# Two layers of attention and feed-forward on one core: the first chunk's q goes to its token layout inside the chip, and the loads behind it are re-ordered

## The reference

```
xn = layernorm(x)
x  = x + attention0(xn) + lora_experts(xn)     # layer 0
xn = layernorm(x)
x  = x + attention1(xn) + swiglu(xn)           # layer 1

attention0: q = xn @ Wqkv[:, :512]  (32 heads of 16), k and v of one shared head
            scores = q.k * scale + slope[h] * (pos_k - pos_q), causal
            out = softmax(scores) @ v  @ Wo
lora_experts: top 2 of 4 gates, rank 16
attention1: within a token, a 16 x 16 softmax of q (sum over heads) and k
swiglu:    (silu(xn @ gate) * (xn @ up)) @ down,  512 -> 1792 -> 512,
           gate, up and down are int32 weights with a scale per row
```

## Time and profile before

| | |
|---|---|
| Time, three runs | median 625.92 us (625.88 to 626.74) |
| Span of the profiled execution | 623.2 us; no separate time of that execution is given, so what lies around the span is taken from the median: 2.7 us |
| PE busy | 570.7 us (92%) |
| DVE, ACT, POOL busy | 461.3, 377.0, 351.7 us |
| Granted clock of PE, mean | 0.959 |
| DMA moved | 34.97 MB in 98942 packets |

### The profile page before, as it was taken

The page is one execution under the profiler, slowest core; times in us unless marked ns, Lnnn a source line. Parts: engine busy times, 40 slices in busy tenths (PEclk is TensorE's granted clock), DMA queues, the critical chain, the costliest instruction groups (busy, mean ns, idle before and its releaser), DMA issues.

```text
span 623.2 us, 14286 instructions
## 1 busy us (share of the span) xinstructions
PE 570.7 (92%) x5590; PEld 421.3 (68%) x5590; DVE 461.3 (74%) x1034; ACT 377.0 (61%) x703; POOL 351.7 (56%) x364
## 2 busy tenths in 40 slices
PE   4579583699999999999999999999999999999997
PEld 4466451467885668776968587858685876785783
DVE  4769874899999874899697748996986569354642
ACT  3287095847875478675757485858684776651240
POOL 6231595724655667674837574848576677542140
PEclk9987895599999999999999999999999999999999
DMA  8767799905054146001610160016001000000000
GB/s 207 152 95 78 123 237 217 170 2 54 2 54 87 37 68 70 3 4 35 88 17 5 35 86 4 4 35 88 1 5 52 18 1 9 28 2 2 35 1 34
DMA packets 98942, 34.97 MB, mean 56 GB/s; under 512 B 75548, under 2 KB 90044, under 8 KB 98876
## 3 DMA queue, kind: packets, MB, share of 16 engines
q1 hardware_dynamic: 76044, 24.58, 22.7%
q0 software_dynamic: 2352, 7.18, 5.7%
q10 hardware_dynamic: 20480, 2.31, 2.6%
HBM read 30.19 MB, written 8.39 MB: 62 GB/s over the span
## 4 chain that ended last, share of the span: by engine, by line
PE 68%; DVE 13%; SPq 8%; ACT 4%; issue 3%; DMA 2%; POOL 2%; ACTq 1%; DVEq 0%
PE B_bank L1266 27%; PE B_bank L1287 14%; PE A_bank L1218 7%; SPq L693 5%; PE A_bank L1191 4%; DVE mx L1537 4%; PE A_bank L1120 3%; PE E_bank L1176 3%; PE B_bank L1154 3%; PE E_bank L1171 2%; PE B_bank L1254 1%; DMA qq<-nmp 1%; ACTq L693 1%; SPq L731 1%; SPq L717 1%
## 5 line engine op out<-in xcount | busy, mean ns | idle before, releaser
L883 POOL TENSOR_TENSOR probs<-e,probs 128x512 f16<-128x512 f32 x176 | 208.3, 1188 | 127.2 <-ACT probs L999 126.8
L1266 PE MATMUL B_bank<-xs,wgu 128*128 128x256 f16 x1792 | 204.3, 273 | 0.3 <-DVE hf L1649 0.3
L998 ACT ACTIVATE e<-E_bank,wn 128x512 f32<-128x512 f32 x192 | 133.7, 696 | 103.4 <-PE E_bank L1176 53.9
L1266 PEld LDWEIGHTS B_bank<-xs,wgu 128*128 128x128 f16 x1792 | 172.7, 98 | 21.6 <-DVE hf L1649 0.6
L999 ACT ACTIVATE probs<-E_bank,wn 128x512 f16<-128x512 f32 x192 | 134.0, 698 | 0.0
L1287 PE MATMUL B_bank<-wd,hbuf 128*128 128x512 f16 x448 | 99.9, 379 | 0.1
L897 POOL TENSOR_TENSOR hbuf<-hf,hbuf 128x512 f16<-128x512 f32 x56 | 65.8, 1176 | 56.2 <-ACT hbuf L1033 55.8
L1537 DVE TENSOR_REDUCE mx<-B_bank 128x2 f32<-128x384 f32 (+5 forms) x168 | 92.1, 603 | 4.5 <-PE B_bank L1154 4.4
L1639 DVE SCALAR_TENSOR_TENSOR hf<-ebuf,B_bank 128x512 f32<-128x512 f32 x56 | 38.3, 684 | 62.2 <-ACT ebuf L1043 61.9
L1287 PEld LDWEIGHTS B_bank<-wd,hbuf 128*128 128x128 f16 x448 | 43.2, 98 | 49.3 <-POOL hbuf L897 0.6
L1043 ACT ACTIVATE ebuf<-B_bank,sgx 128x256 f32<-128x256 f32 x112 | 47.5, 485 | 22.1 <-PE B_bank L1266 20.8
(11 more groups left out here) (199 smaller groups left out, 696.3 us busy)
## 6 DMA issues: line engine op xcount, KB each, us to landing
qq<-q_parts SPq DMA_DIRECT2D x21, 256.0 KB
x<-in_x SPq DMA_DIRECT2D x20, 256.0 KB, 3.1
out_y<-x SPq DMA_DIRECT2D x16, 256.0 KB, 2.0
xa<-in_x SPq DMA_DIRECT2D x12, 256.0 KB, 5.1
q_parts<-qs SPq DMA_DIRECT2D x48, 64.0 KB, 2.9
wgu<-in_gate_w POOLq DMA_DIRECT2D x4, 448.0 KB, 9.1
wgu<-in_up_w POOLq DMA_DIRECT2D x4, 448.0 KB, 8.7
wd<-in_down_w POOLq DMA_DIRECT2D x4, 448.0 KB, 7.1
```

What stands on the lines that cost most here:

```text
L883: pool.tensor_tensor(probs[:, u % PSLOTS, 1, :], e32[:, w, :], probs[:, u % PSLOTS, 0, :], ALU.subtract).then_inc(s_lop, 1)
L998: act.activation(e32[:, w, :], psum("exp", i, g, w)[:, :], ACT.Exp, scale=wn[:, 7:8])
L1266: mm = pe.matmul(psum(name, u, i)[:, a * SEQ:(a + 1) * SEQ].rearrange("p (t n) -> p t n", t=NU), wgu[:, m, k, (2 * i + a) * P:(2 * i + a + ...
```

## The change: what it does

1. **q of the first chunk** is no longer written to DRAM and read back. Four staging tiles `natural[m]` (64 rows x 2048 columns f16, placed in buffers that are idle at that time: `wd`, `hf`, `attnT`, two slots of `x1`) hold one tile m of eight heads in the order (head, token). SP's `place(b, m)` copies three 64 KB pieces from `q_first` into rows 0 to 47 by DMA inside the chip, and DVE's `place(b, m)` copies 64 rows x 2048 columns into `qq`.
2. **Bias and zero rows** of the staging tiles are filled once: DVE's `zero` clears rows 32 to 63 in four memsets ahead of everything else, `consts` loads the tables in 512-byte runs, ACT (not DVE) scales them in `tables`, SP's `tables` puts them into rows 48 to 53 of the four tiles. ident_b is no longer loaded; the f16 identity is made from the f32 one. `clear` on POOL is now a DVE memset.
3. **Maxima of batch 0** are taken in 32 groups in the order of the tiles m (`FIRST_MAXG`), so that each tile's groups start when it is placed. They no longer go into rows of `qq`: `nm0` turns them in two halves, and each `exp` step of batch 0 adds them by four more matmuls of 128 columns, a one-hot row (`pick`) against `nm_first`.
4. **Waits**: `x_load(1)` is planned behind `place(0, 3)` on SP, `wo` behind `place(1, 3)`; `ffn_load(0)` and `late(2)` wait until all eight tiles are placed; `gate` of unit 0 waits for the eight gate and up loads alone, `half` for the four of down. `x1_load` 4 and 5 wait for the placing too. wtok is split ahead of wq (`HI_ORDER`).
5. **Plan**: all costs in `US` and the whole table `RANK` are new, so every engine's order changes from beginning to end. ACT does one small exponential (`warm`) at its start.

```diff
+FIRST_MAXG = [(tb, 2 * n, 2) for n in range(NK) for tb in range(NTB)]
+HI_ORDER = [NK, 0, 1, 2, 3] + list(range(NK + 1, 2 * NK + 2))
...
-            p.add("PE", ("exp", i, g, w), *([sp("nm", i, gap=2.8)] if g == w == 0 else []))
+            p.add("PE", ("exp", i, g, w), *([] if w else [dve("nm0", 0, g // 4)] if i == 0 and g % 4 == 0 else [sp("nm", i, gap=2.8)] if i and g == 0 else []))
...
-    p.add("SP", ("x_load", c), *([pe("q", c - 1, NK - 1)] if c > 1 else [sp("wo", gap=0.0)] if c else []))
+    p.add("SP", ("x_load", c), *([pe("q", c - 1, NK - 1)] if c > 1 else [sp("place", 0, NK - 1, gap=0.0)] if c else []))
...
-        p.add("SP", ("wo",), sp("consts", gap=0.0))
+        p.add("SP", ("wo",), sp("place", 1, NK - 1, gap=0.0))
...
-        p.add("ACT", ("store", b, m), dve("q0", b, m))
+        p.add("SP", ("place", b, m), dve("q0", b, m), *([] if b else [sp("tables", gap=0.0)]), *([dve("place", 0, m)] if b else []))
+        p.add("DVE", ("place", b, m), sp("place", b, m, gap=2.5))
...
+        natural = [wd[:, NB * NK:NB * NK + NK, :].rearrange("p i n -> p (i n)"), hf[:, :, :].rearrange("p a n -> p (a n)").bitcast(F16),
+                   attnT[:, :, :, :].rearrange("p a k t -> p (a k t)"), x1[:, NT:XSLOTS, :].rearrange("p a n -> p (a n)").bitcast(F16)]
...
+            def place(b, m):
+                if b:
+                    sp.wait_ge(s_placed, m + 1)
+                for g, part in enumerate(PART_Q):
+                    if part == 0:
+                        sp.wait_ge(s_q0h, b * NK + m + 1)
+                    else:
+                        wait_used(sp, "q0", b, m)
+                    sp.dma_start(natural[m][g * HD:(g + 1) * HD, :].rearrange("d (h t) -> d h t", t=SEQ),
+                                 q_first[:, b, m, part, :]).then_inc(s_natural[m], 16)
...
             def ffn_load(n):
                 k = n // 2
                 if n == 0:
-                    pool.wait_ge(s_gather[1], 16 * 3)
+                    pool.wait_ge(s_placed, 2 * NK)
...
+                    for c1 in range(0 if i else blocks):
+                        row = g // 2 % 2 * 2 * NTB + 2 * (t0 + c1) + g % 2
+                        mm = pe.matmul(acc[:, c0 + c1, :, :], pick[:, row:row + 1].broadcast_to([NG, P]),
+                                       nm_first[:, g // (NHG // 2), :].rearrange("r (h t) -> r h t", t=GT), start=False, stop=True,
+                                       skip_group_check=True)
...
+            def zero():
+                for m in range(NK):
+                    dve.memset(natural[m][R_ZERO:R_HOT, :].bitcast(F32), 0.0).then_inc(s_zero, 1)
...
+            def place(b, m):
+                dve.wait_ge(s_natural[m], 32 + 48 * (b + 1))
+                dve.tensor_copy(qq[0:R_HOT, b, :, 8 * m:8 * m + 8, :],
+                                natural[m][0:R_HOT, :].rearrange("d (h c t) -> d c h t", c=NTB, t=GT)).then_inc(s_placed, 1)
```

More of the change, by code:

```diff
@@ new lines, in groups_of @@
+def groups_of(i):
+    return MAXG if i else FIRST_MAXG
+US = {"PE": {"norm": 1.1, "norm2": 0.2, "nmT": 0.15, "nm0": 0.25, "q0": 2.0, "xT0": 0.5, "tok": 2.0, "kT": 0.24, "qa": 1.3,
+             "q": 1.3, "pv": 0.62, "attT": 0.46, "midT": 0.13, "outa": 1.3, "out": 1.74, "xT1": 0.46, "tok1": 1.0,
+             "gate": 1.76, "up": 1.76, "half": 1.74, "half2": 1.74, "half3": 1.74, "down": 0.87},
+      "ACT": {"squares": 0.7, "squares2": 1.2, "hi": 1.36, "nmT": 0.3, "nm0": 0.27, "midT": 0.28, "start": 4.6,
+             "tables": 3.4, "q0": 0.4, "xT0": 0.5, "q": 0.5, "kT": 0.75, "mix": 0.12, "exp": 1.16, "attT": 0.5,
+             "xT1": 0.5, "att2": 0.54, "gate": 0.74, "up": 0.54},
+      "DVE": {"zero": 4.2, "norm": 0.2, "scale": 1.3, "tables": 2.94, "place": 0.7, "nm0": 0.3, "scaled": 0.4, "hot": 0.64,
[4 rows of a table added]
+      "POOL": {"norm": 1.0, "norm2": 0.6, "lo": 1.2, "setup2": 2.2, "start": 2.2, "turn": 1.1, "ffn_load": 0.62,
+             "ln0": 0.9, "ln1": 0.9, "late": 0.68, "setup1": 0.5, "exp": 1.16, "att4": 2.1, "up": 1.18},
+      "SP": {"wo": 1.4, "x_load": 2.4, "consts": 3.3, "tables": 5.0, "q": 0.5, "gather": 2.1, "place": 1.85, "nm": 1.2,
+             "x1_load": 0.5, "down": 0.5}}
@@ L223, in run @@
                 del queues[e][step[0]]
-            end[e, step] = free[e] = t + cost(e, step) * (1.1 if e == "PE" and 40 < t < 100 else 1.0)
+            end[e, step] = free[e] = t + cost(e, step) * (1.15 if e == "PE" and 25 < t < 110 else 1.0)
             orders[e].append((t, step))
@@ L291, in attention @@
                 after += [pe("pv", v // NHG, v % NHG)]
-            if u == 4:
-                after += [dve("hot", 7)]
             p.add("ACT", ("exp", i, g, w), *after)
@@ L408, in plan @@
     p.add("POOL", ("start",))
+    p.add("DVE", ("zero",))
     for n in range(N_FFN):
-        p.add("POOL", ("ffn_load", n), sp("gather", 1, gap=8.0), at=34.0 + 5.0 * n)
+        p.add("POOL", ("ffn_load", n), *([dve("place", 1, NK - 1)] if n == 0 else [pool("late", 8)] if n >= 2 * NK else []))
     for c in range(NCH):
@@ L423, in plan @@
             p.add("DVE", ("scaled",), dve("scale"))
-            p.add("DVE", ("tables",), sp("consts"))
-            p.add("SP", ("tables",), dve("tables"))
+            p.add("DVE", ("tables",), at=7.0)
+            p.add("ACT", ("tables",), sp("consts"))
+            p.add("SP", ("tables",), act("tables"), pool("start"), dve("zero"))
             for n in range(8):
@@ L436, in plan @@
                 p.add("DVE", ("scale2", n), pool("norm2", n), dve("scale"))
-            for n in range(10):
-                p.add("ACT", ("hi", n), dve("scale") if n < NK else dve("scale2", 0 if n == NK else 1))
+            for n, part in enumerate(HI_ORDER):
+                p.add("ACT", ("hi", n), dve("scale") if part < NK else dve("scale2", 0 if part == NK else 1))
                 p.add("POOL", ("lo", n), act("hi", n))
             p.add("DVE", ("setup0",), pool("late", 1, gap=6.0))
-            p.add("DVE", ("setup1",), pool("late", 8, gap=8.0), dve("nmT", 0))
+            p.add("DVE", ("setup1",), pool("late", 8, gap=20.0), dve("place", 1, NK - 1), dve("nm0", 0, 1))
             p.add("POOL", ("setup1",), dve("setup0"))
@@ L910, in start, with tables @@
                 act.dma_start(tri_sb[:, :, :], tri).then_inc(s_tri, 16)
+                act.wait_ge(s_init, 1)
+                act.activation(warm[:, :], mhalf[:, 0:1], ACT.Exp)
+            def tables():
+                act.wait_ge(s_rows, 96)
+                act.activation(pos_half, pos_nat, ACT.Copy)
+                act.activation(slope_up, slope_nat, ACT.Copy, scale=POS).then_inc(s_pos, 1)
             def squares(m):
```

322 lines of the change are left out of this document (160 added, 162 removed), and 27 rows, old and new, of tables (RANK, US).

## The result

The kernel after takes 640.08 us (median of 4 runs, 639.61 to 640.84), the one before 626.12 (4 runs): a ratio of 1.0223, interval 1.0209 to 1.0238. The change makes the kernel 14 us slower where 612 was forecast. The profiled execution took 640.21 us, with a span of 638.3.

What follows compares the result with a forecast made beforehand. PE's own work bounds 140 to 600 us; nearly all gain lies before, in idle time and slow clock. Idle -15.7, slow clock -5.8, one-hot +7.3 make -14.2: span 609.0, plus 2.7 gives 611.7, said as 612 us (594 to 628).

Steps and rivals of the forecast that it cites:

- POOL's loads wait for all eight tiles, which I put at 50: Start of POOL's weight loads: all eight q tiles placed at 50 us, leaving SP held until about 98.
- the loads' 35.5 us of all engines: POOL's queue: 7.18 MB in 2352 packets take all DMA engines 35.5 us.
- The 13 us for the stores: SP's 16 stores of the second chunk's q, meeting the loads: 13 us at 12.7 ns a packet.
- the slower rival: SP's hold behind POOL's loads outlasts the earlier one, deciding at 112 us, where time is 632; range 628 to 640, chance 0.15.
- First scores: First score group for batch 0's maxima on PE: at 28.5 us instead of 49.24, 6 us after the scale.
- First exponential: Batch 0's exponentials start after two placed tiles, at about 41 us instead of 77.78.
- Idle ahead of 40 us: PE idle from 0 to 40 us: 16.2 less 5.6 of ACT's held queue plus 1 for `zero`, 11.6.
- 80 to 120: PE idle in this window: 16.8 becomes 13 us, the rest of SP's hold.
- Slow clock: Loss from PE's reduced clock: 11 us instead of 16.8, since the longest gaps shrink.
- One-hot matmuls: 96 matmuls of 128 columns adding batch 0's maxima on PE: +7.3 us, range 0 to 14.6.
- The forecast of 10 us more on DVE: DVE's work over the whole kernel: about 10 us more than before.
- one rival: DVE's list sets the pace and earlier exponentials only wait for it: 623 us (620 to 628), chance 0.11.

Runs made afterwards that it cites:

- e1: Kernel after with POOL's twelve loads of layer-1 weights cut to 128 columns each: 632.80 us, ratio 1.0112.
- e5: Kernel after with its first 30 us reordered on DVE, ACT and POOL, nothing added or left out: 634.69 us, ratio 1.0133.
- e13: Kernel after changed as in e12, and also without batch 0's one-hot matmuls: 621.85 us, ratio 0.9945.
- e12: Kernel after with reordered start, batch 1's maxima turned early, batch 2's maxima later, POOL's loads cut to 128 columns: 625.86 us, ratio 1.0004.
- b2: Kernel before with POOL's nine first loads moved behind later exponential groups and SP's batch 1 maxima ahead of x1: 626.66 us, ratio 1.0017.
- e7: Kernel after with gate and up loads early at 17 us, batch 1's maxima turned early, start reordered: 634.70 us, ratio 1.0135.

## Why the prediction was wrong

**The step that failed is a date.** "POOL's loads wait for all eight tiles, which I put at 50" was 73, and "the second chunk's q comes, at about 55" was 92.8. SP was rid of the stores at 124.30, not at 98. One term under this date was right: the loads' 35.5 us of all engines, whose packets moved for 35.3 us (76.8 to 112.2). That the whole stretch agrees too, 48 us from the first load to the end of the stores (50 to 98) against 50.9 (73.41 to 124.30), is luck: I had 16 stores follow the loads in one go, while eight met their last 20 us and the other eight went out behind them, when the q slots were free again. The 13 us for the stores were taken too high in any case: 12.7 ns a packet is the mean of ACT's whole queue, which without its stores still has 3840 packets at 0.9% of the span in the kernel after, and that leaves some 10 ns a packet and 10 us for the 16 stores.

By the slower rival's own rule, an end at 124.3 instead of 112 gives 632 + 12.3 = 644; measured 640. So the side I gave 0.15 came true, but its mechanism only in part, and that the number comes near is luck as well: with the hold taken away and nothing else changed (e1) the kernel still takes 632.8, and of the 20.8 us by which idle time exceeds the forecast 9.1 lie ahead of 40 us, before any of these loads. That the rival was not taken more seriously is the fault of its condition: I compared 98 with 112 without asking how sure the 50 and 55 were.

**Why these dates were late.** First scores: forecast 28.5, measured 36.8; 4.4 us of it is the later scale: I had priced `zero` alone and not the new order of DVE and ACT around it. The other 3.9 is that from the scale to the first scores it took 9.9 us, not 6. First exponential: 41 forecast, 50.3 measured. Behind that, batch 1's q and tiles stand in the lists between maxima and exponentials, so tiles come one by one until 73. The second x is asked for at 53.2, not 33, and wo at 66.7, not 45. That the second chunk's lateness by itself costs the rest is argued from these dates: in the nine kernels of the table whose stores take under 11 us, the first gate comes 67 to 73 us behind the first of them, whatever else was moved. No run brought that chunk forward alone, and e5 shows only that an earlier start is passed on nearly whole (5.7 us at the scale, 4.7 at the gate).

**The sum, term by term.** Idle ahead of 40 us: 11.6 forecast, 20.7 measured (+9.1). 40 to 80: 4 and 4.5. 80 to 120: 13 and 12.7. The rest: 8.2 and 19.7 (+11.5), nearly all from 120 to 140, where my own forecast had said that SP's list would long be free. Slow clock 11 and 15.9 (+4.9), since the longest gaps moved instead of shrinking: 12.5 of it ahead of 140 us and 3.4 behind, where the kernel before has 0.2. One-hot matmuls 7.3 and 11.0 of work (+3.7); the row that I took, eight of 128 columns in 0.61 us, does not price the short groups in which they run here, four in 0.39 us or two in 0.28. Together these terms make up the 29.3 us between the span of 609.0 and the 638.3 measured; 20.8 of them are idle time. What the one-hot matmuls cost in time was the other case that I named, nothing while PE waits: 1.0 us, and 4.0 with the waits gone.

**What was not consistent.** I put the gate of unit 0 at 110 to 120 and the span at 609. With 471.9 us behind the gate in the kernel before, the two exclude each other by some 20 us; setting them side by side would have shown that the dates were too early. Batch 0's exponentials "over at 41 + 24 x 1.14 = 68" failed likewise: the second half of batch 0's maxima was not ready until 82, and the exponentials stood from 72 to 85 and again for the q slot, to 118.

**What held.** `zero` took 4.1 us in four memsets of 0.91 us, within 2.9 to 4.6, and moved the first layer norm from 3.80 to 5.16, 1.4 us where I said at most 1. The Trainium skill (VectorE: DVE Perf Modes, section "Zero memsets can be issued as uint32 (trn2)") says that a memset takes one cycle an element whatever the type. The prediction's estimate by it, 4.3 us, is near the 4.1 measured; no run here has a memset of a smaller type on this engine. The long stretch from 200 to 600 gave 1.2 us. The forecast of 10 us more on DVE did not hold: 459.5 us against 461.3. Nor does DVE set the pace, as one rival had it: it idles 40.6 us ahead of 140 us, 4.7 more than before.

**What the runs tell of the 14 us.** The start's order gave back 5.4, the maxima behind the reads 5.4, the loads 7.3, the one-hot matmuls 1.0, each alone. These four add up to 19.1, and all of them together, with the later maxima of batch 2, give back 18.2 (e13); but that agreement is chance. Without the one-hot part (e12) 14.2 come back where the three add up to 18.1, since each only shifts the date of the same gate until the next wait binds, and the one-hot matmuls then give 4.0 instead of 1.0. e13 is 3.8 us better than the kernel before, but with loads and matmuls left out. With nothing left out the best is 629.7, still 0.9% slower than before. The 13 us of idle time that e13 keeps from 80 to 120 have no one cause.

## What to carry to other kernels

Moving the first consumer earlier wins nothing if the date that binds (here the first gate) hangs on a chain that moved later; find that date in the profile first, and check every forecast date against it. In these kernels the stretch in which bulk loads filled the DMA engines charged one wanted transfer, whichever came next; reordering the list behind it changed who paid. So put the loads where nobody waits, or make them smaller, and look for late landings as well as held issues. Undo parts together as well as singly: waits in series hide each other, and work hidden in a wait has its price only when the wait is gone.

## What the runs showed of the hardware

The issue of a transfer on SP, not only its landing, can be held while POOL's loads run, and also for very small transfers: two of batch 1's maxima took 11.29 us in b2, 10.65 of it one issue, where the median issue of that line is 0.59. Not every issue is held. In the kernel after the first two stores were issued in 0.38 and 0.58 us at 92.82 and 93.24, and the third took the 15.67; in e7 six tile transfers were issued from 25.04 to 28.95, in the middle of the loads, in 0.59 to 0.66 us each. A store moves 1040 packets, a tile transfer 144, but whether the number of packets that wait decides was not tested. The store that took longest to land in the kernel after took 20.2 us, with cut loads 5.0. The Trainium skill (DMA: Bandwidth & Descriptors, section "Queues, rings and completion order") says that each DMA engine takes turns between the queues packet by packet. The long landings agree with it; that the issuing queue stops too is shown by these rows alone.

Early loads at 15 to 17 us, in a stretch that without them has a DMA share of 0.09 (20 to 40 us in the kernel after), were not free either. They did not hold the issue of the transfers inside the chip, but they delayed their landing: DVE stood 8.71 us for the first tile in e7, and 0.26 in the kernel after.
